# Attention with gated linear state: the normalised rows of blocks 8 to 31 turned by DMA instead of on TensorE

## What is computed

```python
h = _layernorm(x) * (1 + ca) + sa
# attention half, H = 4 heads of 128
q = silu(h @ wq); k = sigmoid(h @ wk); v = h @ wv; f = 1 - k
theta = cumsum(sign(f - 0.5)) * pi
qr, kr = concat(q cos, q sin), concat(k cos, k sin)
S = S * exp(log f) + kr v^T ;  o = (qr * scale) S     # scan over the 4096 rows
out = layernorm_rms(o * sigmoid(h @ wg1 @ wg2)) * norm_w @ wo
x = x + ga * out
h = _layernorm(x) * (1 + cb) + sb
# FFN half: mixes each row with the one before it
x = x + gb * sigmoid(xr @ W_r) * (square(relu(xk @ W_k)) @ W_v)
```

## Time and profile before

| | |
|---|---|
| median of 3 runs | 1782.2 us (1780.37 to 1782.49) |
| the profiled execution | 1780.5 us, its span 1778.9 us |
| granted TensorE clock | 0.999 |
| TensorE busy | 1760.4 us, 99% |
| VectorE busy | 1521.7 us, 86% |
| ScalarE busy | 829.3 us, 47% |
| GpSimd busy | 364.1 us, 20% |

### The profile page before, as it was taken

The page is one execution under the profiler, slowest core; times in us unless marked ns, Lnnn a source line. Parts: engine busy times, 40 slices in busy tenths (PEclk is TensorE's granted clock), DMA queues, the critical chain, the costliest instruction groups (busy, mean ns, idle before and its releaser), DMA issues.

```text
span 1778.9 us, 45434 instructions
## 1 busy us (share of the span) xinstructions
PE 1760.4 (99%) x18909; PEld 1583.8 (89%) x18909; DVE 1521.7 (86%) x3483; ACT 829.3 (47%) x1493; POOL 364.1 (20%) x303
## 2 busy tenths in 40 slices
PE   9999999999999999999999999998999999999999
PEld 7888989989999899989999899977889898989888
DVE  7898989989899899989898889998777778787875
ACT  4444444444444544444444544444454545445453
POOL 1000111101110111101110111102434343434443
PEclk9999999999999999999999999999999999999999
DMA  6122113211221112311121112211221211111110
GB/s 237 49 61 60 38 37 80 54 37 38 43 66 38 37 39 58 98 38 37 43 67 37 38 38 55 55 49 47 73 72 48 72 52 68 60 60 60 60 60 36
DMA packets 107700, 102.02 MB, mean 57 GB/s; under 512 B 65748, under 2 KB 67560, under 8 KB 107496
## 3 DMA queue, kind: packets, MB, share of 16 engines
q1 hardware_dynamic: 107480, 99.11, 19.6%
q10 hardware_dynamic: 16, 0.00, 0.0%
HBM read 48.77 MB, written 34.60 MB: 47 GB/s over the span
## 4 chain that ended last, share of the span: by engine, by line
PE 94%; DVE 5%; issue 1%; ACT 0%; DVEq 0%; ACTq 0%
PE bank L1341 64%; PE lvl L1341 9%; PE bank L1448 3%; PE bank L1349 3%; PE bank L1455 3%; PE bank L1447 3%; PE lvl L1416 3%; PE bank L1439 1%; PE lvl L1399 1%; PE lvl L1434 1%; PE lvl L1428 1%; PE bank L1674 0%; PE bank L1667 0%; DVE xk L1000 0%; DVE K L931 0%
## 5 line engine op out<-in xcount | busy, mean ns | idle before, releaser
L133 POOL TENSOR_TENSOR ln_rs<-ln_ve,mhalf 128x2 f32<-128x2 f32 x64 | 82.8, 1293 | 865.5 <-DVE ln_ve L128 865.5
L1341 PE MATMUL bank<-hT_hi,wq_hi 128*128 128x256 f32 x512 | 148.2, 289 | 1.4 <-DVE hT_lo L759 1.2
L407 POOL COPY og_halves<-og 128x1024 uint16<-128x1024 uint16 x60 | 65.6, 1093 | 407.5 <-DVE og L956 407.5
L1341 PE MATMUL bank<-hT_hi,wk_hi 128*128 128x256 f32 x512 | 148.2, 289 | 0.0
L1341 PE MATMUL bank<-xk_hi,fk_hi 128*128 128x256 f32 x512 | 145.1, 283 | 0.6 <-DVE xk_lo L1013 0.6
L1341 PE MATMUL bank<-hT_hi,wq_lo 128*128 128x256 f32 x512 | 144.9, 283 | 0.0
L1341 PE MATMUL bank<-hT_lo,wk_hi 128*128 128x256 f32 x512 | 144.9, 283 | 0.0
L1341 PE MATMUL bank<-xk_hi,fk_lo 128*128 128x256 f32 x512 | 144.9, 283 | 0.0
L1341 PE MATMUL bank<-xk_lo,fk_hi 128*128 128x256 f32 x512 | 144.9, 283 | 0.0
L1341 PE MATMUL bank<-hT_lo,wq_hi 128*128 128x256 f32 x512 | 144.8, 283 | 0.0
L1341 PE MATMUL bank<-hT_hi,wk_lo 128*128 128x256 f32 x512 | 144.7, 283 | 0.0
(11 more groups left out here) (234 smaller groups left out, 5754.0 us busy)
## 6 DMA issues: line engine op xcount, KB each, us to landing
xs<-in_L_attn_x SPq DMA_DIRECT2D x32, 512.0 KB, 3.9
x_scratch<-xs SPq DMA_DIRECT2D x32, 512.0 KB, 3.4
xs<-x_scratch SPq DMA_DIRECT2D x32, 512.0 KB, 3.6
out<-xs SPq DMA_DIRECT2D x31, 512.0 KB, 2.8
mod_raw<-in_L_wmod SPq DMA_DIRECT2D x6, 1024.0 KB, 7.3
raw_q<-in_L_attn_wq SPq DMA_DIRECT2D x2, 512.0 KB, 4.9
raw_k<-in_L_attn_wk SPq DMA_DIRECT2D x1, 1024.0 KB, 5.8
raw_v<-in_L_attn_wv SPq DMA_DIRECT2D x1, 1024.0 KB, 6.7
```

The lines of the kernel that those rows point to most:

```text
L133: pool.tensor_tensor(out=ln["rs"][:, :], in0=ln["ve"][:, :], in1=mhalf[:, :], op=ALU.pow).then_inc(ln["rstd"], 1)
L407: pool.tensor_copy(halves[:, ch, :].rearrange("p (two e) -> p two e", two=2), og[n % 2][:, ch, :].bitcast(U16).rearrange("p (e two) -> p t ...
L1341: last = pe.matmul(dst, lhs(a, s), rhs(b, s), start=(t == 0), stop=(t == len(terms) - 1))
```

## The change

For blocks 8 to 31 the eight products with the identity are left out. In their place:
- GpSimd splits the two chunks of `xn` in halves (`xn_split`), behind `ln_rstd`; SyncE turns them with two transposing DMAs (`turn_rows`), ahead of `turn_og(n, 0)`; ScalarE joins the halves in `hF` (`h_join`), ahead of the turned keys, and applies scale and shift to `hF` in place (`h_scaled`), where `h_affine` stood.
- VectorE takes statistics and variance of block n + 2 ahead of `f_signed` of pair 0 and normalises right behind it, instead of later in the body. Its scratch in `f_signed` is now the first half of `hF` (in all bodies).
- The load of the raw FFN weight W_r, whose place the new tiles take, moves from body 18 to body 30.

Blocks 0 to 7 and the whole FFN half keep the products with the identity; their counts in the waits are adapted (`pe_before`).

```diff
+FIRST_TURN = 8
+def by_dma(n):
+    return FIRST_TURN <= n < NB
+def dma_before(n):
+    return sum(by_dma(j) for j in range(n))
+def pe_before(n):
+    return n - dma_before(n)
...
+        xn_halves = at("xn_halves", [P, NC, 2 * E], 198, U16)
+        xn_halvesT = at("xn_halves_turned", [P, NC, 2 * KT, P], 202, U16)
...
+                def turn_rows(n, ch):
+                    sp.wait_ge(xn_halved, NC * dma_before(n) + ch + 1)
+                    wait(sp, xn_joined, NC * (dma_before(n) - 1) + ch + 1)
+                    sp.dma_start_transpose(xn_halvesT[:, ch, :, :], xn_halves[:, ch, :]).then_inc(xn_turned[ch], 16)
...
                     if n == BPB + 2:
                         sp.wait_ge(w_lo["o"], 2 * KT)
-                        for name in "kr":
-                            rows_in(raw[name], env["W_" + name], raw_in[name])
+                        rows_in(raw["k"], env["W_k"], raw_in["k"])
                     if n == LAST - 1:
+                        sp.wait_ge(xn_joined, NC * dma_before(NB))
+                        rows_in(raw["r"], env["W_r"], raw_in["r"])
...
+                    if n + 2 < NB and by_dma(n + 2):
+                        for ch in range(NC):
+                            turn_rows(n + 2, ch)
                     if n < LAST - 1:
                         turn_og(n, 0)
...
+                def xn_split(n, ch):
+                    pool.wait_ge(ln["xn_ready"], n + 1)
+                    wait(pool, xn_turned[ch], 16 * dma_before(n))
+                    pool.tensor_copy(xn_halves[:, ch, :].rearrange("p (two e) -> p two e", two=2),
+                                     xn[:, ch, :].bitcast(U16).rearrange("p (e two) -> p two e", two=2)).then_inc(xn_halved, 1)
...
                     ln_rstd(pool, ln, mhalf, n + 2)
+                    if by_dma(n + 2) and n + 2 < NB:
+                        for ch in range(NC):
+                            xn_split(n + 2, ch)
...
+                def h_join(n, ch):
+                    act.wait_ge(xn_turned[ch], 16 * (dma_before(n) + 1))
+                    act.wait_ge(h_lo, n)
+                    act.wait_ge(f_sb, 2 * n)
+                    act.copy(hF[:, :, :].bitcast(U16).rearrange("p k (c t two) -> p c two k t", c=NC, two=2)[:, ch],
+                             xn_halvesT[:, ch, :, :].rearrange("p (two k) t -> p two k t", two=2)).then_inc(xn_joined, 1)
+                def h_scaled(n):
+                    act.wait_ge(xn_joined, NC * (dma_before(n) + 1))
+                    for k in range(KT):
+                        act.activation(hF[:, k, :], hF[:, k, :], ACT.Identity, scale=scl[0][:, n // BPB, k:k + 1],
+                                       bias=sft[0][:, n // BPB, k:k + 1]).then_inc(h_full, 1)
...
                     g1_high(n + 1)
+                    if by_dma(n + 2) and n + 2 < NB:
+                        for ch in range(NC):
+                            h_join(n + 2, ch)
                     for ch in range(chunks_kept(n)):
                         keys_turned(n, ch)
...
-                        h_affine(n + 2)
+                        if by_dma(n + 2):
+                            h_scaled(n + 2)
+                        else:
+                            h_affine(n + 2)
...
-                    dve.wait_ge(mm["t1"], 2 * (n + 2))
-                    f_signed(n + 1, 1 - par, 0, xn[:, 0, :])
+                    dma = by_dma(n + 2) and n + 2 < NB
+                    spare = hF[:, 0:2, :].rearrange("p k t -> p (k t)")
+                    if dma:
+                        ln_stats(dve, ln, n + 2)
+                        ln_var(dve, ln, n + 2)
+                    f_signed(n + 1, 1 - par, 0, spare)
+                    if dma:
+                        apply_next(n + 2)
...
                     level_update(n, par, 32, 4)
-                    f_signed(n + 1, 1 - par, 1, xn[:, 0, :])
+                    f_signed(n + 1, 1 - par, 1, spare)
...
                     q_odd(n + 1, 1 - par)
...
-                    ln_stats(dve, ln, n + 2)
-                    ln_var(dve, ln, n + 2)
+                    if not dma:
+                        ln_stats(dve, ln, n + 2)
+                        ln_var(dve, ln, n + 2)
...
-                    apply_next(n + 2)
+                    if not dma:
+                        apply_next(n + 2)
...
-                    t1(n + 2)
+                    if not by_dma(n + 2) or n + 2 >= NB:
+                        t1(n + 2)
```

More of the change, by code:

```diff
@@ L260, in blocks @@
                                                "fk", "fr", "fv")}
+        xn_halved, xn_joined = (sem(ctx, n) for n in ("xn_halved", "xn_joined"))
+        xn_turned = [sem(ctx, f"xn_turned{n}") for n in range(NC)]
         h_full, q_sig, k_f, v_sb, g1_hi, gate_sb, kt_sb, ogt_hi, merged_act, qf_sb = (
@@ L467, in h_affine @@
                     act.wait_ge(h_lo, n) if n > 0 else None
+                    act.wait_ge(f_sb, 2 * n) if n > 1 else None
                     for k in range(KT):
                         if k % 2 == 0:
-                            act.wait_ge(mm["t1"], 2 * n + k // 2 + 1)
+                            act.wait_ge(mm["t1"], 2 * pe_before(n) + k // 2 + 1)
                         src = bank[5 - 5 * (k // 2)][:, (k % 2) * TB:(k % 2 + 1) * TB]
                         act.activation(hF[:, k, :], src, ACT.Identity, scale=scl[0][:, n // BPB, k:k + 1],
+                                       bias=sft[0][:, n // BPB, k:k + 1]).then_inc(h_full, 1)
[9 more added lines that the diff above has]
+                        act.activation(hF[:, k, :], hF[:, k, :], ACT.Identity, scale=scl[0][:, n // BPB, k:k + 1],
                                        bias=sft[0][:, n // BPB, k:k + 1]).then_inc(h_full, 1)
@@ L478, in h2_affine @@
                         if k % 2 == 0:
-                            act.wait_ge(mm["t1"], 2 * (NB + m) + k // 2 + 1)
+                            act.wait_ge(mm["t1"], 2 * pe_before(NB + m) + k // 2 + 1)
                         last = act.activation(h2[:, k, 1:TB + 1], banks[k // 2][:, (k % 2) * TB:(k % 2 + 1) * TB], ACT.Identity,
@@ L1033, in apply_next @@
                 def apply_next(n):
-                    dve.wait_ge(mm["t1"], 2 * n)
+                    dve.wait_ge(mm["t1"], 2 * pe_before(n))
+                    wait(dve, xn_halved, NC * dma_before(n))
                     ln_apply(dve, ln, n)
```

## The result

The changed kernel takes 1792.38 us (median of 4 runs, 1791.21 to 1793.65) against 1781.31 us for the kernel before on the same chip: a ratio of 1.0064, 95% interval 1.005 to 1.0078. It is slower by 11 us; the forecast was 1791.8. Its profiled execution has a span of 1789.5 us, 10.6 more than before, at the same clock of 0.999.

A forecast was written before the change was run, and what follows sets the result against it. TensorE, busy 99%, was taken as the bound. Waits of 0.62 + 23 x 1.09 + 4.8 = 30.5 us less 20.9 gave +9.6: 1780.5 to 1790.1, raised 1.7 to the runs' median, 1791.8 us; range 1768 to 1806.

The forecast's parts named there:

- The gain: TensorE in bodies 6 to 29 loses the transposes of one block each: 24 x 0.87 = 20.9 us.
- The loop through `q_odd`: From VectorE's line 867 through `q_odd` and the near scores to the next 867: 19.88 + 16.85 = 36.73 us.
- The order without contention: VectorE's moved work in body 18 without GpSimd stalls: `q_odd` ends at 727.66, before TensorE comes at 728.81.
- The holds: GpSimd's two new copies each stall VectorE ahead of `q_odd` by 0.86 us, 1.72 in sum; bounds 0 and 2.08.
- The step from TensorE's release: From the end of VectorE's `q_odd` to TensorE's near scores: 0.05 us, estimated from a 0.04 us TensorE-to-VectorE step.
- Which instructions are held: GpSimd's copies were to stall VectorE instructions right behind the normalisation: lines 928, 931 and 783.
- Power and wait of the normalisation: VectorE's normalisation needs GpSimd's power: no wait taken, bounds 0 and 0.7 us.
- Extra products: `gate_wo2` in bodies 12 to 15 and four wo products in body 17, ahead of `q_odd`: 8 x 0.60 = 4.8 us.
- ScalarE and the DMAs: Transposes land 3.1 us after issue; two joins of 1.36 us end about 732.8, ahead of the keys; no cost.
- The sum: Whole kernel: TensorE's new waits before the near scores, 30.5 us, less 20.9 saved: +9.6 us.
- A loose reading: Attention bodies before the change: a period of 36.51 us in nearly all, only those round the batch boundary shorter.
- the first: Rival: TensorE stays the bound; 1763 us without VectorE stalls (chance 0.12), 1771.6 with one of the two (0.15).

The follow-up runs named there:

- the version with late copies: Changed kernel with GpSimd's two copies held until `q_odd` is done and ScalarE's two joins moved behind the gates: 1768.10 us, ratio 0.9932.
- the last version: Changed kernel with copies after `q_odd`, joins behind the gates, block 19 keeping TensorE's transposes, `gate_wo2` behind the variants: 1762.66 us, ratio 0.9898.
- the run with the order alone: Kernel before with only VectorE's new order in bodies 6 to 29 and the new scratch; no copies or DMA transposes: 1783.10 us, ratio 1.0015.
- The run with late joins: Changed kernel with only ScalarE's two joins moved behind the gates, copies left in place: 1796.27 us, ratio 1.0087.
- the run with one copy and one fill: Changed kernel with GpSimd's copy of chunk 0 kept and that of chunk 1 replaced by a fill with zeros: 1774.94 us, ratio 0.9971.
- the run with two fills: Changed kernel with both GpSimd copies replaced by fills with zeros that read nothing from SBUF: 1773.02 us, ratio 0.9958.
- late copies alone: Changed kernel with only GpSimd's two copies held until `q_odd` is done, joins left ahead of the turned keys: 1770.37 us, ratio 0.9938.

## Why the prediction was right

- **The gain.** 24 x 0.87 us of TensorE left, as counted (the body of the version with late copies, 35.65 us, is 0.86 shorter than 36.51); with the holds out of the way most of it came back as time (the last version: 17.8 us less than before, of 20.0 for its 23 blocks).
- **The loop through `q_odd`.** Forecast: `q_odd` ends 19.83 us behind the mark, 0.05 to TensorE, 16.85 from there to the next mark, a body of 36.73. Measured in body 18: 738.03 - 718.40 = 19.63, then 0.26, then 755.21 - 738.29 = 16.92: 36.81. The order without contention was forecast at 727.66 - 709.55 = 18.11; the run with the order alone gave 18.11.
- **The holds were a little too dear.** 0.86 us each from line 866; the new copies cost 0.72 each. The step from TensorE's release was too cheap: 0.05 was taken between a TensorE product and VectorE, but from VectorE to the near scores it is 0.26. The two errors nearly cancel (1.44 + 0.26 = 1.70 against 1.72 + 0.05 = 1.77), which is luck.
- **Which instructions are held was wrong.** The prediction named 928, 931 and 783 as the first behind the normalisation. The record of the first copy starts at 733.59, but lines 989, 992 and 844 ran at their full pace; as I read it, the copy got in only in the short wait between 844 and 846. It changed nothing in the sum, since 846 and 853 are ahead of `q_odd` as well.
- **Power and wait of the normalisation.** No wait was taken, between bounds of 0 and 0.7: line 139 follows 846 at 732.51, a slot of 0.64 instead of 0.60. Right.
- **Extra products.** Bodies 12 to 14 rose by 0.6 us over their neighbours (37.38 to 37.40 us against 36.8), as forecast. Body 17 rose by 3.9, not by 2.4: the missing 1.5 us are TensorE at half clock (below).
- **ScalarE and the DMAs.** The joins are done at 742.25 + 1.38 = 743.6, later than the forecast 732.8 on the old scale (which is 741.6 here), for two reasons. The second copy ends 0.5 us late (737.49; the forecast 728.1 is 736.95 here), and the second transpose lands 4.7 us after its issue instead of 3.1. Such slow landings, 4.5 to 5.0 us, come in 9 of the 24 bodies; why, no run shows. The turned keys follow at once (743.49), and TensorE, which needs them at 746.17, waits for nothing. The run with late joins confirms it.

```profile
742.25 1.38 ACT L521 COPY hF<-xn_halves_turned 128x1024 uint16<-128x1024 uint16 x1 [1.63 <-DMA xn_halves_turned<-xn_halves]
743.49 1.05 ACT L610 COPY Kt<-bank 128x512 f32<-128x512 f32 x2
```

- **The sum.** From the marks of body 6 to that of the crossing the changed kernel took some 12.5 us more, 3 more than the 9.6 forecast: 1.5 for the clock in body 17, 0.05 to 0.1 in each ordinary body, and 0.4 in each of bodies 9 and 19, where a wait of VectorE between the two state updates, there before too, is no longer hidden. Behind the crossing's mark it was 1.7 us shorter (588.1 against 589.8), and the clock shows why: in the crossing TensorE waits for VectorE (busy for 1.11 of 3.70 us before), behind that its clock fell to half in the execution of the kernel before, and twelve products took 4.47 us; in the execution of the changed kernel it stayed full, and they took 2.97. The first two rows are of before, the third of the changed kernel:

```profile
1202.74:1206.15 3.41, 3.41 (x21) 2.19 (x23) 0.88 (x2) 2.50 (x7) 0.00 (x0) 0.50 0.41 154
...
1201.59 4.47 PE bank L1341 x12
...
1213.83 2.97 PE bank L1411 x12
```

- **Luck in the total.** Such a stretch comes and goes between runs of one kernel: those of the kernel before took 1779.3, 1780.5 or 1782.1 us, at mean clocks of 1.000, 0.999 and 0.998. Here it hid 1.7 of the extra 3 us, and the 1.7 us by which the forecast was raised from 1790.1 to 1791.8 are the same scatter. What the prediction owes to its mechanism is the body of 36.73 (36.81 measured).
- **A loose reading.** Not only bodies round the batch boundary differ from 36.51 us before: bodies 0 to 2, 5 and 30 take 37.4 to 41.4. None of them is in the sum.

Of the rivals, the first describes the other runs, if roughly: with one hold less the gain is 5.5 us (10.6 was given), with the holds out of the way and the rest covered 17.8 (19.1 was given). That the times nearly agree there, 1762.7 against 1763, is luck: the rival counted 24 blocks and a loss in body 17, and started from 1782.2.

What stays open: why GpSimd's copy had to sit out three VectorE instructions in a row in the changed kernel (733.59 to 735.18), but came in between lines 865 and 866 at once, and between 905 and 981 in the version with late copies. No run isolated this.

## What to carry to other kernels

Before an engine's work is taken off a bound engine, look in the order of its neighbour for the instruction that the bound engine waits for, and count what is put ahead of it, the stalls included: here it was 2 us more in a body, in front of one 0.7 us product, and it outweighed 0.87 us of saved TensorE. A GpSimd copy costs VectorE a hold per instruction, so place it where VectorE waits anyway (here behind `q_odd`), or cut it small. Small extras that only some bodies carry need a cover of their own, once the common one is used up.

## What the hardware showed that was not expected

**A wait of some 3 us cost more than itself.** Body 17 of the changed kernel: TensorE waits 2.77 us for `q_odd`, and then the near scores take 1.51 us instead of 0.89, the wo product 3.88 instead of 2.95. Stretches of that kernel, with busy time of each engine and the granted clock behind it (columns: window, length, PE, PEld, DVE, ACT, POOL busy with counts, PEclk, DMA share, GB/s), then the chain:

```profile
696.90:699.90 3.00, 0.27 (x20) 0.11 (x8) 2.96 (x3) 1.33 (x4) 2.24 (x2) 1.00 0.35 69
699.90:704.00 4.10, 4.06 (x71) 3.47 (x72) 4.07 (x9) 1.37 (x2) 0.00 (x0) 0.58 0.44 82
```
```profile
699.94 1.51 PE lvl L1469 x64
701.45 3.88 PE bank L1411 x12
```

The granted clock falls from the level of 2.4 GHz to a mean of 0.58, so for most of 4 us to that of 1.2 GHz, after 3 us with TensorE busy for 0.27. It costs 1.5 us on top of the wait. In the run with one copy and one fill a wait of 2.05 us at the same place was followed by a full clock (its near scores took 0.89 us), in the run with two fills one of 1.89 us by a mean of 0.68. The length of the last wait alone doesn't decide it. Two runs with the same wait show this best: with late copies and late joins, and with late copies alone, TensorE waits 1.34 us for `q_odd` in body 17, and the near scores then take 1.51 us in the first and 0.89 in the second:

```profile
688.63 1.51 PE lvl L1470 x64
...
689.29 0.89 PE lvl L1470 x63
```

In the first, TensorE had also waited 1.14 us at the level product 2 us earlier (0.20 in the second). That this earlier wait made the difference is not shown.

**Short instructions can be the dearest.** Line 981 of the version with late copies works on 8 columns, 0.16 us by itself, and took 0.99 us beside a GpSimd copy. A hold does not scale with the instruction that is held, but with the one that holds: 0.71 to 0.86 us from a copy of 1024 elements, 0.29 from one of 512 (0.41 in one place), 0.55 from a fill of 1024.
